# The causal bar of an attention kernel: from unit-matrix products to 43 further contraction rows

## The reference, cut to what matters

```python
xn = layernorm(x)
Q, K, V = relu(xn @ Wq + bq), relu(xn @ Wk + bk), relu(xn @ Wv + bv)   # 16 heads, dh = 8
scores = einsum('bqhd,bkhd->bhqk', Qh, Kh) / sqrt(8)
scores = where(key_mask == 0, NEG, scores)
scores = where(tril == 0, NEG, scores)              # the causal bar: key > query gets -2**32
attn = softmax(scores) ; out = einsum(attn, Vh) + xn ; s = layernorm(out)
g = silu(feed_forward(xn))
return x + s * g
```

## Time and profile before

| | us |
|---|---|
| device time, median of 3 runs | 506.54 (504.40 to 506.75) |
| profiled execution, span from first to last instruction | 504.5 |
| its launch-to-end time | not given apart from the span; the lowest run is 504.40 |
| PE busy | 443.9 (88%) |
| DVE busy | 379.8 (75%) |
| ACT busy | 302.3 (60%) |
| POOL busy | 171.9 (34%) |
| DMA | 37.62 MB, 27,514 packets, mean 75 GB/s |

### The profile page before, as it was taken

How to read it: one execution, slowest core, us unless ns; L and a number is a source line. 1 busy time by engine, 2 the same in 40 slices (tenths; PEclk the granted TensorE clock), 3 DMA queues, 4 the chain that set the end, 5 groups by cost and what they waited for, 6 DMA issues and landing times.

```text
span 504.5 us, 10471 instructions
## 1 busy us (share of the span) xinstructions
PE 443.9 (88%) x3799; PEld 272.5 (54%) x3799; DVE 379.8 (75%) x889; ACT 302.3 (60%) x644; POOL 171.9 (34%) x439
## 2 busy tenths in 40 slices
PE   0059978999999899999999999999999999999870
PEld 0036744777777555555555555555555555555430
DVE  6997989688882496779779769769769778778507
ACT  0145623888888246666666666666666666666760
POOL 8031032111110310211471481481471472372293
PEclk9996999999999999999999999999999999999995
DMA  8900203234443303123123222222222222230000
GB/s 241 307 0 9 77 0 87 64 113 115 114 122 84 91 1 97 52 53 90 55 70 85 62 71 73 63 78 65 82 54 72 79 67 71 63 84 24 3 23 21
DMA packets 27514, 37.62 MB, mean 75 GB/s; under 512 B 5686, under 2 KB 19910, under 8 KB 27462
## 3 DMA queue, kind: packets, MB, share of 16 engines
q1 hardware_dynamic: 27302, 36.92, 26.4%
q0 software_dynamic: 160, 0.03, 0.0%
HBM read 25.91 MB, written 10.49 MB: 72 GB/s over the span
## 4 chain that ended last, share of the span: by engine, by line
PE 50%; DVE 10%; POOL 2%; issue 2%; ACT 1%; DVEq 0%; ACTq 0%; POOLq 0%
PE banks L1048 14%; PE banks L1079 13%; PE banks L1067 11%; DVE mx L893 5%; PE banks L1050 5%; PE banks L1069 5%; DVE stats L940 1%; PE banks L1089 1%; PE banks L1133 1%; DVE aggr L944 1%; ACT pt L1014 1%; ACT ots L998 0%; DVE seed L72 0%; DVE bits L71 0%; PE banks L1057 0%
## 5 line engine op out<-in xcount | busy, mean ns | idle before, releaser
L893 DVE TENSOR_REDUCE mx<-banks 128x1 f32<-128x384 f32 (+3 forms) x384 | 210.2, 597 | 63.5 <-PE banks L1050 57.7
L1014 ACT ACTIVATE pt<-banks 128x512 f32<-128x512 f32 (+2 forms) x384 | 184.4, 527 | 102.1 <-PE banks L1069 90.5
L1050 PE MATMUL banks<-causal,ident_b 128*128 128x128 bf16 x512 | 102.7, 220 | 0.0
L1069 PE MATMUL banks<-causalT,ident_b 128*128 128x128 bf16 x512 | 102.3, 219 | 0.0
L1079 PE MATMUL banks<-pt,vg 128*18 128x512 f32 (+3 forms) x1024 | 81.4, 436 | 1.3 <-ACT pt L1014 1.3
L1048 PE MATMUL banks<-w_room 73*128 73x512 bf16 (+3 forms) x256 | 69.0, 302 | 3.4 <-DVE mx L893 3.4
L1048 PE MATMUL banks<-k_own,q_own 73*128 73x512 bf16 (+3 forms) x256 | 69.2, 302 | 3.0 <-DVE mx L893 2.5
L1067 PE MATMUL banks<-w_room 76*128 76x512 bf16 (+3 forms) x256 | 67.7, 300 | 1.5 <-ACT pt L1014 1.5
L1067 PE MATMUL banks<-q_own,k_own 76*128 76x512 bf16 (+3 forms) x256 | 68.5, 300 | 0.2 <-ACT pt L1014 0.2
L793 POOL TENSOR_SCALAR mneg<-mx 128x16 f32<-128x16 f32 x32 | 8.1, 252 | 168.7 <-DVEq L901 168.7
L1050 PEld LDWEIGHTS banks<-causal,ident_b 128*128 128x128 bf16 x512 | 50.2, 98 | 0.9
(11 more groups left out here) (170 smaller groups left out, 638.9 us busy)
## 6 DMA issues: line engine op xcount, KB each, us to landing
k_scratch<-parts SPq DMA_DIRECT2D x40, 128.0 KB, 2.4
q_own<-q_scratch SPq DMA_DIRECT2D x48, 96.0 KB
k_own<-k_scratch SPq DMA_DIRECT2D x48, 96.0 KB
w_room<-q_scratch SPq DMA_DIRECT2D x48, 96.0 KB
w_room<-k_scratch SPq DMA_DIRECT2D x48, 96.0 KB
q_scratch<-parts SPq DMA_DIRECT2D x24, 128.0 KB, 2.4
w_room<-in_w_dram SPq DMA_DIRECT2D x1, 2048.0 KB, 9.1
out_dram<-mixed SPq DMA_DIRECT2D x7, 256.0 KB, 2.3
```

The costliest lines, as they stand in the source:

```text
L893: ins = dve.tensor_reduce(mx[:, u % 2, heads[0]:heads[-1] + 1, q], banks[:, S0 + c % RING, 0:w * len(heads)].rearrange("p (h k) -> p h k", ...
L1014: act.activation(weights(k, heads[0], len(heads)), banks[:, ST0 + j % RING, 0:(T - P * k) * len(heads)], ACT.Exp, scale=SCALE).then_inc(ex ...
L1050: ins = mm(o[:, w - P:w], ident_b[:, :], causal[:, :], start=False, stop=True)
L1069: ins = mm(o[:, 0:P], ident_b[:, :], causalT[:, :], start=False, stop=True)
```

## The change

The bar becomes part of the contraction. 43 further rows (`BLOCKS` = 43, one for each 3 positions of a 128-block) are added to both stacks, below row 76: `bar_k` and `bar_q`, step functions of the position within the block whose products are 0 on the allowed side and hugely negative on the barred one. A diagonal block is now one product over 119 rows (`STACK`), the columns off the diagonal one over 76 rows (`LIVE`); there is no unit-matrix product. The two bars are made by POOL in the first part (`bar_rows`), and copied from SBUF to SBUF into all 16 heads of each stack by `load_fixed`, in place of `load_ones`. Since `chunk` now reads rows 73 to 75 too, these must be zero in `qx` until the maxima come: `q_fixed` (a row of ones and three of zeros) is stored to `q_scratch` behind the parts of Q by one more DMA a batch, and comes with the third load of a group.

```diff
@@ load_queries
-        src = q_dram[bass.ds(b, 1), :, :, G * g:G * g + G, :].rearrange("b p d h t -> (b p d) (h t)")
         for r in range(PARTS):
+            n = QROWS if r == PARTS - 1 else PARTS * DH
+            src = q_dram[bass.ds(b, 1), 0:n, G * g:G * g + G, :].rearrange("b r h t -> (b r) (h t)")
...
-    def load_ones(sp, par):
-        sp.dma_start(qx[par][MROW:MROW + 1].rearrange("p g h t -> p (g h) t"),
-                     ones_b[0:1, :].unsqueeze(1).broadcast_to([1, HEADS, T])).then_inc(ones_in[par], 16)
-        sp.dma_start(kx[par][MROW + 1:STACK].rearrange("p g h t -> p (g h) t"),
-                     ones_b[:, :].unsqueeze(1).broadcast_to([PARTS, HEADS, T])).then_inc(ones_in[par], 16)
+    def load_fixed(sp, par):
+
+        sp.dma_start(kx[par][MROW + 1:LIVE].rearrange("p g h t -> p (g h) t"),
+                     ones_b[:, :].unsqueeze(1).broadcast_to([PARTS, HEADS, T])).then_inc(fixed_in[par], 16)
+        for stack, bar in ((kx[par], bar_k), (qx[par], bar_q)):
+            sp.dma_start(stack[LIVE:STACK].rearrange("p g h t -> p (g h) t"),
+                         bar[:, :].unsqueeze(1).broadcast_to([BLOCKS, HEADS, T])).then_inc(fixed_in[par], 16)
...
@@ SP, first part
+                        if o == 0:
+                            sp.dma_start(q_dram[i:i + 1, PARTS * DH:QROWS].rearrange("b r h t -> (b r) h t"),
+                                         q_fixed[:, :].unsqueeze(1).broadcast_to([1 + PARTS, HEADS, T])).then_inc(
+                                             parts_out[i % 2][0], 16)
                     if i == 1:
-                        load_ones(sp, 0)
+                        sp.wait_ge(bars_ready, 1)
+                        load_fixed(sp, 0)
...
                 sp.wait_ge(w2_done, B)
-                load_ones(sp, 1)
+                load_fixed(sp, 1)
@@ POOL, first part
-                pool.memset(causal[:, :], 0.0).then_inc(blank, 1)
-                pool.memset(causalT[:, :], 0.0).then_inc(blank, 1)
+                pool.memset(q_fixed[:, :], 0.0).then_inc(blank, 1)
...
+                def below(bar, k, value, sign=1):
+
+                    link(pool.affine_select(out=bar[:, :].rearrange("p (n t) -> p n t", t=P),
+                                            in_=bar[:, :].rearrange("p (n t) -> p n t", t=P),
+                                            compare_op=ALU.is_ge, fill=value, base=-k * sign,
+                                            pattern=[[0, TB], [sign, P]], channel_multiplier=-BLOCK * sign))
+
+                def bar_rows():
+
+                    link(pool.memset(bar_k[:, :], BAR_KEYS[BLOCK]))
+                    for k in range(BLOCK, 0, -1):
+                        below(bar_k, k, BAR_KEYS[k - 1])
+                    link(pool.memset(bar_q[:, :], BAR_QUERIES[BLOCK - 1]))
+                    for k in range(BLOCK - 1, -1, -1):
+                        below(bar_q, k, BAR_QUERIES[k - 1] if k > 0 else 0.0)
+                    below(bar_q, BLOCK - 1, 0.0, -1)
+                    pool.sem_inc(bars_ready, 1)
...
                     if i == 0:
                         second_roots(tok, GROUPS[0])
+                        bar_rows()
@@ PE, chunk (keys has the same change, with the sides swapped)
-                        mm(o, qx[by][0:MROW + 1, g, h, P * q:P * q + P], kx[by][0:MROW + 1, g, h, 0:w],
-                           start=True, stop=False)
-                        ins = mm(o[:, w - P:w], ident_b[:, :], causal[:, :], start=False, stop=True)
+                        if q > 0:
+                            mm(o[:, 0:w - P], qx[by][0:LIVE, g, h, P * q:P * q + P], kx[by][0:LIVE, g, h, 0:w - P],
+                               start=True, stop=True)
+                        ins = mm(o[:, w - P:w], qx[by][0:STACK, g, h, P * q:P * q + P],
+                                 kx[by][0:STACK, g, h, w - P:w], start=True, stop=True)
```

More of the change, by code:

```diff
@@ L39 @@
 MROW = SPLIT
-COPIES = (PARTS, 2 * PARTS - 1)
+LIVE = MROW + 1 + PARTS
+BLOCK = 3
+BLOCKS = -(-P // BLOCK)
+STACK = LIVE + BLOCKS
+QROWS = PARTS * DH + 1 + PARTS
+BAR_KEYS = (0.0, 2.0 ** -37, 2.0 ** 13, 2.0 ** 63)
+BAR_QUERIES = (-2.0 ** 62, -2.0 ** 12, -2.0 ** -38)
+STORES = (PARTS + 1, 2 * PARTS - 1)
 BIG = 2.0 ** 100
@@ L120, in build_program @@
     ident_b = sb("ident_b", [P, P], BF16)
-    causal = sb("causal", [P, P], BF16)
-    causalT = sb("causalT", [P, P], BF16)
+    bar_q = sb("bar_q", [BLOCKS, T], BF16)
+    bar_k = sb("bar_k", [BLOCKS, T], BF16)
+    q_fixed = sb("q_fixed", [1 + PARTS, T], BF16)
     rows_sb = sb("rows_sb", [P, 4, C])
     half = sb("half", [P, 2, C])
-    STACK = MROW + 1 + PARTS
     UNIT_DMAS = 16 * (2 * PARTS + 1)
@@ L253, in _ @@
                         sp.wait_ge(low_ready, tok.next(low_ready))
-                        for k in range(COPIES[o]):
-                            dst = (q_dram, k_dram)[o][i:i + 1, k].rearrange("b d h t -> (b h) d t")
+                        for k in range((PARTS, 2 * PARTS - 1)[o]):
+                            part = k_dram[i:i + 1, k] if o == 1 else q_dram[i:i + 1, DH * k:DH * k + DH]
+                            dst = part.rearrange("b d h t -> (b h) d t")
                             sp.dma_start(dst, parts[:, i % 2, o, k % PARTS, :]).then_inc(parts_out[i % 2][o], 16)
+                        if o == 0:
+                            sp.dma_start(q_dram[i:i + 1, PARTS * DH:QROWS].rearrange("b r h t -> (b r) h t"),
+                                         q_fixed[:, :].unsqueeze(1).broadcast_to([1 + PARTS, HEADS, T])).then_inc(
+                                             parts_out[i % 2][0], 16)
                     if i == 1:
-                        load_ones(sp, 0)
+                        sp.wait_ge(bars_ready, 1)
+                        load_fixed(sp, 0)
                     if 2 <= i < 2 + NG:
@@ L276, in _ @@
                 pool.memset(bias_rows[:, :, :], 0.0).then_inc(blank, 1)
-                pool.wait_ge(blank, 7)
+                pool.memset(q_fixed[:, :], 0.0).then_inc(blank, 1)
+                pool.wait_ge(blank, 6)
+                pool.memset(q_fixed[0:1, :], 1.0).then_inc(blank, 1)
                 for t in (ident, ident_b):
@@ L348, in _ @@
                     pool.sem_inc(stack_in[0][g], 16)
[L350 removed]
+                pool.sem_inc(blank, -10)
             @block.vector
@@ L535, in split @@
                         stored = parts_out[i % 2][o]
-                        act.wait_ge(stored, tok.next(stored, 16 * COPIES[o]))
+                        act.wait_ge(stored, tok.next(stored, 16 * STORES[o]))
                         act.activation(full[:, o, :], banks[:, QB + o, :], ACT.Relu, bias=bias)
@@ L1066, in keys @@
                         o = banks[:, ST0 + j % RING, n * i:n * i + n]
[L1067 to L1069 removed]
+                        if k < TB - 1:
+                            mm(o[:, P:n], kx[par][0:LIVE, g, h, P * k:P * k + P],
+                               qx[par][0:LIVE, g, h, P * k + P:T], start=True, stop=True)
+                        ins = mm(o[:, 0:P], kx[par][0:STACK, g, h, P * k:P * k + P],
+                                 qx[par][0:STACK, g, h, P * k:P * k + P], start=True, stop=True)
                     ins.then_inc(st_done, 1)
@@ L1111, in batch @@
                                 if first and (g, c) == (2, 0):
-                                    pe.wait_ge(ones_in[1], 32)
+                                    pe.wait_ge(fixed_in[1], 48)
                                 if c == 0:
@@ L1125, in batch @@
                         outputs(tok)
-                pe.wait_ge(ones_in[0], 32)
+                pe.wait_ge(fixed_in[0], 48)
                 tok = Tokens(pe)
@@ L1132, in _ @@
                         chunk(tok, 0, u, c)
-                        mm(banks[:, ST0 + RING - 1, :], qx[0][0:MROW + 1, u, 0, 0:P], kx[0][0:MROW + 1, u, 0, :],
+                        mm(banks[:, ST0 + RING - 1, :], qx[0][0:LIVE, u, 0, 0:P], kx[0][0:LIVE, u, 0, :],
                            start=True, stop=True)
```

25 lines of the change are left out of this document (9 added, 16 removed).

## The result

| | before | changed kernel |
|---|---|---|
| median of the runs | 506.44 us | 592.92 us (591.12 to 593.91) |
| ratio | | 1.172, 95% interval 1.168 to 1.176 |
| profiled execution, span | 504.5 us | 592.2 us |
| first product of the second part | 172.38 us | 245.53 us |
| first keys | 184.78 us | 279.47 us |

The kernel is 17% slower; the forecast was 625 us, range 545 to 715. The first keys come 94.7 us later, and the rest takes 7.0 us less.

A forecast was written before the change was run, and what follows sets the result against it. PE (busy 37.82 of 38.67 us a batch) was taken to bound the second part. First keys at 326 us plus 319.7 minus 24 gave 622; 2 for the median and 1 for the clock made 625 us, range 545 to 715.

The forecast's parts named there:

- The price of a packet: Bar copies in load_fixed: a lone DMA engine takes 0.060 us per 1 KB packet, ends 0.053 and 0.125.
- D: Time of a pair of bar copies on one DMA engine: 1376 packets x 0.060 = 83 us (73 to 172).
- the working of the first load: First part: copies start at 96.5 us, stores land behind them, ACT's K split of i = 4 moves by 63 us.
- SP isn't held, the keys wait for the DMA: Start of second part: PE's first keys wait for the maxima's DMA behind the second bar copies, and come at 319 us.
- The second part begins 4 us before the end: If SP is held by the second bar copies, ending at 318 us, the first keys come at 328 us.
- PE's gain: Second part: diagonal blocks lose 128 columns each; a batch saves 3.3 us (38.67 to 35.4), 24 us in all.
- The plain group of 7.9 us: Second part: a group without other work, scheduled from the end of chunk 1, takes 7.9 us against 9.13.
- The one that I gave 9.0: Second part, group 0: DVE's other work and POOL's floor leave a gain of only 0.1 us.
- The two that I let gain 2.8 together: Second part: the plain group falls from 9.13 to 7.9 us, and group 2 saves 1.6 us.
- the group with DVE's extra work, given 9.7: Second part, group 1: DVE has 3.9 us of other work, so the group gains only 0.5 us.
- POOL: 7.5 us taken: First part: bar_rows' two memsets and seven selects ahead of totals(0) take 7.5 us (4.9 to 9.5), delaying everything behind.
- Costs nothing further: The added q_fixed stores, the 28-row load and the wait fixed_in add no time; SP issues 8 us of DMAs in 13.7.

The follow-up runs named there:

- the two edits that removed or filled them: On the 48-row kernel with bar_rows called earlier: DVE's statistics pieces later and further apart, 506.1 us; unit-matrix products back for group 3's maxima, 510.5 us.
- the combined version: Changed kernel with 48-row bars, earlier bar_rows, spread statistics, second load_fixed in the second part, POOL's pieces in three groups, 20 idle products: 480.6 us, 0.950 of before.

## Why the prediction was right, and where its sizes were not

The direction, the mechanism and its place were right: the bars' copies run on one engine, in both places, and ACT's split of batch 4 and PE's first keys are what they delay. 48 rows against 47 shows it. The 625 us were 32 too many, from two terms with opposite signs: 50 too many for the copies, 17 too few for PE. Each alone would have left the forecast inside its range (575 or 642 us); that they cancel in part is luck.

- **The price of a packet: 0.060 taken, 0.0422 measured.** D is 58.1, not 83; twice the difference is 50 us. The bounds, 0.053 and 0.125, did not hold it either. Both came from rows in which several engines work at once, and a time per packet worked out from a busy share contains what they cost one another: the same copies spread over 16 engines show 0.089. That a lone engine has no one to share with was in the text, but only moved the value to the near end. The Trainium skill, page "DMA: Bandwidth & Descriptors", sections "Why small descriptors are slow (HBM only)" and "Where 436 GB/s comes from", would have given it: 32 beats of 32 bytes and 3 more per packet, at 850 MHz, an estimate of 0.041 us. The trace agrees with 0.0422, though this is a copy from SBUF to SBUF, for which the first section denies the overhead (without the 3 beats the estimate is 0.038).
- **What is hidden.** With D = 58.1 the working of the first load gives a shift of ACT's split by 39 us; 41.4 were measured. Of the second, the branch "SP isn't held, the keys wait for the DMA" came true in its result, with SP held all the same (26 us): its hold is only half of the copy, and the prologue of the second part ran beside the other half. "The second part begins 4 us before the end" was wrong: it began 34 us before the first keys.
- **PE's gain: 24 us taken, 7.0 measured**, 17 us. This is the step that failed. A steady batch saves 1.0 us, not 3.3. The plain group of 7.9 us was right only where DVE and POOL have less to do (7.96 in the first batch, which saves 4.3). The four intervals say where the missing 2.2 us are. The one that I gave 9.0 took 9.66, 0.5 more than before: POOL's chain begins at the end of DVE's group, and PE, now early, waits 1.54 us in full. The two that I let gain 2.8 together gained 2.2 (9.69 to 8.52 and to 8.67). And the group with DVE's extra work, given 9.7, took 10.78 with the fall of the clock in it, 9.18 without: the fall, for which the sum had nothing outside the two restarts, costs 1.6 us, more than the 1.0 won there. Batches in which the clock did not fall, in the version with 48 rows, took 36.0 us, against 37.1 to 37.6 with one short fall. (It was 38.5 in two batches in which it was low for longer.) That products at half the clock are what lengthens the group is shown; that the waits bring the fall about is supported by the two edits that removed or filled them, and not settled, since the fall then often came elsewhere, and the same wait of 0.86 us had a fall behind it in two batches of seven only. Counted from transpose to transpose, the seven batches together saved 11.1 us; 2.6 of it were lost between the first keys and the third transpose, with the clock at 0.50 and then 0.70, and 1.5 behind the last of these batches, whose group had a fall as well.
- **POOL: 7.5 us taken, 6.6 for the nine instructions**, the selects 0.74 and 0.73 us each; second_norm moved by 7.5, since DVE was slowed beside them.
- **"Costs nothing further": wrong**, but hidden. In the versions with 48 rows the stores of q_fixed and SP's longer issues, with the second load_fixed, let PE wait 4.2 to 4.4 us ahead of the second part (0.45 before), and the stretch to the first keys, now at half the clock, takes 18.5 us in place of 12.4. Under the copies none of it showed; with 48 rows these 10 us are more than the time behind the first keys saves (8.5).

With both sizes put right, 456.5 + 2 x 58.1 + 17 is 589.7, against a span of 592.2 (the 1 us that was added for the clock is in the 17).

## What to carry to other kernels

Before a DMA is added, look at the outermost count of both sides: the primes 43 and 47 there put the whole transfer on one engine, where 48 put it on all 16, and what this queue issued later waited behind it; a few unused rows are cheaper. When the bounding engine is relieved, list what the others do between the same two marks, group by group: the gain stops where the next chain begins, and must be made room for by moving that chain. A relieved PE waits more, and the clock can fall behind its waits; read the granted clock per window, not only the busy time.

## What the runs showed of the hardware that was not expected

- One DMA engine alone moved 1 KB packets from SBUF to SBUF every 42.2 ns, 24 GB/s (521 packets in 22 us).
- One issue on SP was held for 26 us behind a copy on one engine, that is until some 600 of the pair's 1376 packets had been moved; the copy's size in packets sets the hold (28.8 us with 47 rows).
- POOL's selects stretched DVE instructions of 0.17 us to 0.54, and four of 1.14 us in all to 2.34.
- The same copies with 48 rows, spread over 16 engines, moved 163 GB/s: each packet kept its engine for 0.089 us.
- PE's granted clock fell to half for some 3.4 us once in nearly every batch of the changed kernel, behind waits of 0.26, 0.50 and 0.61 us; behind a single wait of 0.86 us, in the combined version, it fell in two of seven batches. It was 0.51 and 0.54 over the 18 us behind a wait of 4.4 and of 2.5 us at the start of the second part; with the wait at 0.48 us, and twice the idle products ahead, it was 1.00 there.
